# Look-ups of the first block that wait for the transposes of the tile in front

## The reference

```python
e = jnp.stack([tbl_0[ids[:, 0]], ..., tbl_31[ids[:, 31]]], axis=1)   # 1024 x 32 x 64
p, q = e[:, ROW], e[:, COL]                                          # the 496 pairs
kp = jnp.einsum('bpj,ipj->bpi', p, kernel)                           # kernel: 64 x 496 x 64
z = jnp.sum(kp * q, axis=-1)                                         # 1024 x 496
h = jnp.concatenate([z, dense_ctx], axis=1)
h = jnp.maximum(h @ W_top1 + b_top1, 0.0)                            # 512
h = jnp.maximum(h @ W_top2 + b_top2, 0.0)                            # 256
y = h @ W_top3
```

## Time and profile before

| | us |
|---|---|
| median of three runs | 493.63 |
| profiled execution | 490.83 |
| its span | 489.1 |
| PE busy | 445.8 (91%) |
| DVE busy | 303.2 (62%) |
| ACT busy | 260.7 (53%) |
| POOL busy | 232.3 (48%) |
| look-ups (L417), 244 of them | 231.2 |

### The profile page before, as it was taken

The page is one execution under the profiler, slowest core; times in us unless marked ns, Lnnn a source line. Parts: engine busy times, 40 slices in busy tenths (PEclk is TensorE's granted clock), DMA queues, the critical chain, the costliest instruction groups (busy, mean ns, idle before and its releaser), DMA issues.

```text
span 489.1 us, 10184 instructions
## 1 busy us (share of the span) xinstructions
PE 445.8 (91%) x3421; PEld 249.8 (51%) x3421; DVE 303.2 (62%) x293; ACT 260.7 (53%) x1874; POOL 232.3 (48%) x251
## 2 busy tenths in 40 slices
PE   8469989989998999799998998899999899999997
PEld 4136545545555455355654554555554555564443
DVE  7316567776766677677656775776776878771000
ACT  6026674756656767663566657545586668101122
POOL 6715656566555565556555555556655640000000
PEclk9759999989999999999999999899999999999999
DMA  6145654121018111211121112111121101000000
GB/s 170 42 135 159 195 163 121 21 66 21 19 21 193 23 24 21 66 21 23 20 64 23 25 20 68 20 20 22 24 63 24 21 20 45 0 3 0 0 1 1
DMA packets 18266, 24.31 MB, mean 50 GB/s; under 512 B 6387, under 2 KB 11767, under 8 KB 17958
## 3 DMA queue, kind: packets, MB, share of 16 engines
q1 hardware_dynamic: 10406, 15.64, 10.9%
q0 software_dynamic: 7808, 8.01, 8.4%
HBM read 19.44 MB, written 0.00 MB: 40 GB/s over the span
## 4 chain that ended last, share of the span: by engine, by line
PE 82%; another core or an unknown queue 6%; DVE 6%; issue 3%; ACT 2%; POOL 0%; POOLq 0%; DVEq 0%; ACTq 0%
PE u_ps L688 36%; PE u_ps L709 13%; PE z_ps L722 11%; PE u_ps L769 6%; PE z_ps L728 6%; DVE prod L605 5%; PE t_ps L642 4%; PE u_ps L789 3%; PE u_ps L695 1%; PE z_ps L664 1%; DVE prod L608 1%; DVE pass_prod L616 0%; PE u_ps L631 0%; ACT prod L522 0%
## 5 line engine op out<-in xcount | busy, mean ns | idle before, releaser
L417 POOL DMA_INDIRECT nat<-tbl,ids_sb x244 | 231.2, 947 | 166.7 <-issue 59.0
L605 DVE TENSOR_TENSOR prod<-u_ps,rows 128x1024 f32<-128x1024 f32 x184 | 218.2, 1220 | 106.8 <-PE u_ps L688 53.3
L502 ACT ACTIVATE pass_prod<-pass_prod 128x64 f32<-128x64 f32 x896 | 214.6, 243 | 38.0 <-DVE pass_prod L616 30.4
L688 PE MATMUL u_ps<-rows,k_sb 64*128 64x256 f32 x1472 | 194.3, 395 | 16.6 <-DVE prod L605 9.3
L688 PEld LDWEIGHTS u_ps<-rows,k_sb 64*128 64x128 f32 x1472 | 133.3, 187 | 102.8 <-issue 46.4
L502 ACT ACTIVATION_READ_ACCUMULATOR pass_prod<-pass_prod 128x1 f32 x896 | 169.5, 189 | 3.6 <-issue 3.6
L616 DVE TENSOR_TENSOR pass_prod<-u_ps,nat 128x1024 f32<-128x1024 f32 x56 | 68.1, 1217 | 23.9 <-PE u_ps L709 19.0
L709 PE MATMUL u_ps<-k_sb,rows 64*128 64x256 f32 x448 | 65.1, 408 | 5.7 <-DVE prod L605 3.5
L722 PE MATMUL z_ps<-prod,sel 128*32 128x512 f32 x512 | 69.9, 612 | 0.0
L490 ACT ACTIVATE rows<-t_ps 128x512 f32<-128x512 f32 (+1 forms) x38 | 19.5, 514 | 90.0 <-remote 55.3
L709 PEld LDWEIGHTS u_ps<-k_sb,rows 64*128 64x128 f32 x448 | 43.0, 194 | 22.9 <-DVE prod L605 8.3
(11 more groups left out here) (50 smaller groups left out, 95.8 us busy)
## 6 DMA issues: line engine op xcount, KB each, us to landing
by_self<-rows SPq DMA_DIRECT2D x32, 128.0 KB
nat<-tbl,ids_sb POOLq DMA_INDIRECT x244
k_sb<-kern SPq DMA_DIRECT2D x3, 768.0 KB
k_sb<-kern SPq DMA_DIRECT2D x2, 640.0 KB
k_sb<-kern SPq DMA_DIRECT2D x1, 1152.0 KB
k_sb<-kern SPq DMA_DIRECT2D x2, 512.0 KB
rows<-w SPq DMA_DIRECT2D x1, 1024.0 KB
rows<-tbl SPq DMA_DIRECT2D x4, 224.0 KB
```

What stands on the lines that cost most here:

```text
L417: pool.indirect_dma_start(nat_of(m, n)[:, h * EMBED:(h + 1) * EMBED], None, tables[f], bass.IndirectOffsetOnAxis(ids_sb[:, col:col + 1], 0 ...
L502: op = nc.scalar.activation(of, of, ACT.Copy, accum_out=z_nat[:, b % 2, s, row:row + 1])
L605: nc.vector.tensor_tensor(to, u, by.unsqueeze(1).to_broadcast([P, 2, 2, SIZE]), ALU.mult).then_inc(prod_ready, 1)
L688: op = nc.tensor.matmul(u[:, h, :], k_sb[part, k_of(d), side, :], rows[part, tile, cols_of(b)], start=True, stop=True)
```

## The change

For the tiles 5 to 10 of the first block, POOL's wait in front of the four look-ups becomes another one. Tile 5 had none and now waits until `transposed` stands at 4, that is until tiles 0 and 1 are transposed. Tiles 6 and 7 had none, and tiles 8, 9 and 10 waited for 1, 2 and 3; now tile m waits for m, that is until the tile in front of it is transposed. The waits for pieces and quads stay as they are, and so does everything from tile 11 on.

```diff
 AHEAD = 30
+IN_STEP = {5: 4, 6: 6, 7: 7, 8: 8, 9: 9, 10: 10}
...
                 b, tile = tile_at(m)
-                if m >= LANES:
+                if m in IN_STEP:
+                    pool.wait_ge(transposed, IN_STEP[m])
+                elif m >= LANES:
                     pool.wait_ge(transposed, m - LANES + 1)
```

## The result

The changed kernel takes **495.59 us** (median of 22 runs, 493.0 to 499.57), the kernel before 492.08 us (22 runs, 489.38 to 495.23). The ratio is **1.0064, with a 95% interval of 1.0044 to 1.0083**: about 3.1 us slower by the ratio (the two medians are 3.5 us apart), where the forecast was no change. The profiled execution of the change has a span of 491.2 us, that of before 489.1 us: 2.1 us of the 3.1 are in this pair of traces. Lines of the changed kernel are three higher than before (L417 is L420, L490 is L493, L642 is L645, L688 is L691).

The account below looks back on a forecast made before the run. Bound: PE's counts held while look-ups leave POOL back to back. -12.6 + 6.05 + 5.7 + 1.7 = +0.85 us, less 0.85 for the clock, makes 0: forecast 493.6 us, range 486.5 to 499.5 us.

Parts of the forecast that it names:

- What bounds the kernel: While look-ups leave POOL back to back, PE's counts reach others late, 1.0 to 3.1 us after the run.
- Rival B: Front stall has its own cause, isn't freed, and look-ups lose their cover: 499.7 to 505.4 us; chance 0.14.
- Term (1): Tile 5's wait cuts the first run to eight look-ups; ACT's first copy at 14.9 us, not 27.56: gain 12.6 us.
- Term (2): Tiles 6 to 10 wait for the tile in front, at least 6.5 us from tile to tile: sum +6.05 us.
- PE's own work is longer: 0: Tile 8's step: PE's own work of 7.84 us exceeds the 6.5 us step, so no cost.
- found them hidden: SP's k_sb loads wait for `transposed` three tiles ahead, 19 us at 6.5 us a tile, so they stay hidden.
- Term (3): Behind tile 10's wait, nine look-ups in a run give back 5.7 us; the stretch to tile 11 adds +1.7.
- The clock: A shorter front stall may spare PE 3.3 us at half clock, gaining 1.7 us; half counted, -0.85.
- rival C: PE's clock falls to half in the new pauses, three stretches losing 1.65 us each, +5: 498 us; chance 0.10.
- Rival A: A count slips through amid the nine look-ups, so most of the 6.5 us gain stays: 487.1 us; chance 0.21.

Follow-up runs that it names:

- experiment 2: The change without tile 5's wait, only the waits of tiles 6 to 10 kept: 502.8 us, ratio 1.0208 to the kernel before.
- experiment 13: The change with tile 12's look-ups on tile 13's thresholds, on a fourth chip: 493.63 us, ratio 1.0118 to the kernel before.
- the fills: The change with 35 chained GpSimd fills of an unread buffer ahead of tile 5's wait, on the fourth chip: 493.74 us (one run).
- experiment 1: The change with only tile 5's wait kept, tiles 6 to 10 waiting as before: 488.46 us, ratio 0.9917 to the kernel before.
- experiment 15: The kernel before with tile 6's look-ups issued twice, for a first run of 21, on the fourth chip: 491.57 us, ratio 1.0100.
- experiment 14: The kernel before, unedited, with a profile, on the fourth chip: 487.11 us.
- experiment 4: The change, with tiles 11, 12 and 13 also waiting until the look-ups of the tile in front have landed: 499.47 us, ratio 1.0142 to the kernel before.

## Why the prediction was wrong, step by step

- **What bounds the kernel** (counts held behind back-to-back look-ups): right in the main wherever counts are held; shown by the first run's length in the changed kernel and experiment 2, by the later run's length in experiment 13, and by the fills. Too strong was that counts come out only behind a run (experiments 1 and 15). Rival B, that the front has a cause of its own, fell there.
- **Term (1), the first release:** predicted 14.9 us, measured 14.84. So close a hit is partly luck: the 1.7 us behind the run were chosen between 1.3 and 3.1 us, and the 3.1 was 1.5 us in experiment 14. The gain at tile 5 is 14.3 us against 12.6, and the 1.6 us more are the clock's (below).
- **Term (2), the steps: this is the step that failed.** Five steps were to cost +6.05 us, and they cost 37.60 - 27.79 = **+9.8** (tile 5 to tile 10, now and in the earlier trace rows). Four of them are 6.85, 7.12, 6.96 and 6.98 us where 6.5 was forecast: from a tile's last issue (36.67 us in POOL's timeline, tile 7) to its transposes at 39.10 us it is 2.4 us and not 2.0. That is 1.9 us. The fifth is tile 8, "PE's own work is longer: 0", and took 9.69 us, 1.85 us over that work; together 3.8 us, about as much as the total is off. Tile 8's last look-up starts at 43.56 us, and its transposes at 48.79 us, 5.2 us behind it. From 42 to 46 us the DMA engines are busy for 0.77 and 0.88 of the time, at 217 and 252 GB/s, and SP's timeline of the changed kernel says with what:

```profile
39.99 2.69 SPq L450 DMA_DIRECT2D by_self<-rows  x4
42.72 6.93 SPq L464 DMA_DIRECT2D k_sb<-kern  x2
```

  SP first issues the loads of `by_self`, and so the load of `k_sb` behind them still runs when tile 8's last look-up leaves: the share is 0.88 from 46 to 47 us and 0.07 from 47.0 to 48.8. In the other steps such a load runs too (0.98 from 27 to 29 us, 0.97 from 35 to 36, 0.91 from 52 to 53, 0.87 from 59 to 60), but in the stretch around the last look-up it is over (0.08 from 29 to 30 us, 0.12 from 36 to 37, 0.25 from 53 to 54, 0.19 from 60 to 61), and there PE has the tile 2.4 to 2.5 us behind that look-up. The prediction asked whether SP's loads of k_sb would be late, and found them hidden. It did not ask whom they delay. On the third chip tile 8's step was 10.16 us, with the same loads at 39.85 and 42.57 us. That the loads are the cause is read from these rows; no run took them away.
- **Term (3), the run behind tile 10's wait:** nine look-ups, release at 67.7 us and +5.7 us were forecast; it was eleven, 72.2 us and 72.75 - 62.73 - 2.58 = **+7.4** (2.58 is tile 10 to double 15 before, 69.8 - 67.22). The mechanism is right (experiment 13, and the 9.6 us more than on the third chip), the size was off: the fourth quad, at which POOL was to stop behind the ninth look-up, had got through by the tenth, and double 12's count by the eleventh; POOL stopped at the twelfth, for double 13. What PE waited for last was also another: ACT's copy of tile 10 (72.22 us), and not DVE's product. The stretch after it cost (80.23 - 72.75) - (76.72 - 69.8) = +0.6 and not +1.7. Together (3) was +8.0 for +7.4; the two errors nearly cancel, which is luck.
- **The clock:** -0.85 was counted for the front, half of what the slow stretch there could give. It gave all: the first pass behind the release takes 1.13 us in the row at 19.14 us, and took 2.08 before, the product behind it 3.67 for 4.31, together 1.6 us. But rival C came too, in three stretches at 0.50 to 0.52. In two of them, behind 32.1 and 49.2 us, PE waits for the next landing anyhow; in the third double 15 and the pass behind it take 2.08 and 1.92 us instead of 1.13 and 1.03. The forecast's sum had put that at nothing. These 1.8 us lie behind 72.75 us, so they are all in the +0.6: at full clock that stretch would have been about 1.3 us shorter than before.

The sum at tile 11: -14.3 + 9.8 + 7.4 + 0.6 = +3.5 us, as 80.23 - 76.72. Without the error of (2), 3.8 us, it would be -0.3 us. The pair of traces agrees with the total only roughly. Behind tile 11, where both kernels wait for the same things, the difference falls to 0.6 us at the first transposes of the next block (110.24 for 109.60 us; the slow stretch at 107 us is gone), and later it goes between 0.6 and 3.3 us and ends at 2.1. It is the 22 runs of each kernel, 3.1 to 3.5 us apart, that bear out the 3.5 us at tile 11.

**Rival B's sign holds on other chips.** The prediction took the hold for a property of the kernel. Where it is absent there is no front to free, and the change costs 3.25%, since the look-ups no longer run under PE's work. There the rule of the Trainium skill (DMA: Bandwidth & Descriptors, Rules for kernel authors), issue early and wait late, gives the right sign, and the traces agree: 10.8 us for five waits, 3.7 us for tile 5's. Rival A did not come, although a quad's count did slip through: it made the run longer and not shorter, since it was the count that POOL itself waited for.

What stays open: what makes a chip hold the counts, and why a count can come out inside a long run. No run told that apart. Each set ran on its chip once, so it could also be a condition of that time. Nor does "counts are held" cover all that happens in the front of the kernel before: from 15.45 to 27.51 us PE takes 1.4 to 2.1 us for each half-product of tile 3's product, and most of its idle time there is "issue", so nothing that the profile shows holds it; in the changed kernel the sixteen half-products of 14.00 us take 2.24 us together.

## What to carry to other kernels

A wait put ahead of an engine's queue of transfers does not only cost its own time: the work behind it becomes a debt, and it was paid here in one burst at the first place without a wait (experiments 1, 4 and 13); forecast where the burst lands and what it delays there. When the landing of a transfer is a term of the path, look for the other queue's loads in the same stretch, and ask whom they delay as well as who waits for them. And before tuning against a stall that no row names a cause for, see whether it is there on another chip: here one and the same change costs 0.6% in one place and 3.3% in another, and experiment 1 is a gain of 0.8% on the first and a loss of 0.8% on the third.

## What the runs showed of the hardware that was not expected

- The same program takes 423 us on two chips and 487 to 492 us on two others, a difference of 64 to 69 us. How much of that the held counts explain was not measured. In the slower pair PE's counts reach the others late while look-ups are issued back to back (ACT's first copy at 25.9 us in experiment 14, 27.6 us in the profile before); on the third chip the changed kernel's first copy starts 0.03 us after PE's product. For the changed kernel PE is busy for 438.2 us of 491.2 (89%) in the profile after and 417.6 us of 436.5 (96%) on the third.
- Held counts came out 1.7 and 2.3 us behind the end of runs of eight and twelve look-ups, and 3.1 us (1.5 us in experiment 14) behind one of seventeen. Inside longer runs some came out before the end: 0.2 us in a run of thirteen, 1.3 us in one of eleven, 3.4 us in one of 21, where the next came 3.8 us after the end.
- 9.48 us of fills on the same engine hold nothing (first copy at 14.69 us, 14.84 without them); look-ups do.
- In the changed kernel PE fell to 1.2 GHz after pauses of 3.65 us (ahead of 31.98 us), 2.27 us (ahead of 48.79) and 7.38 us (ahead of 72.75): the granted clock is 0.50 from 32.1 to 35.4 us, 0.52 from 49.2 to 52.6 and 0.51 from 69.65 to 76.5. After a pause of 2.28 us ahead of 39.10 us it stayed at 1.00 (39.1 to 42 us). So the length of the pause alone does not decide it.
- Look-ups whose last one left at a time when SP's load of `k_sb` was under way reached PE 5.2 us behind it (tile 8), the others 2.4 to 2.5 us.
